# A graph network layer on one core: the last tile's packed slots are taken early and singly in one PSUM bank

## The reference

```python
msg = jnp.concatenate([h[src], h[dst]], axis=-1) @ Mw.T + Mb
s1, s2 = segment_sum(msg, dst), segment_sum(msg * msg, dst)
mx, mn = segment_max(msg, dst), segment_min(msg, dst)
mean = s1 / degc
var = relu(s2 / degc - mean * mean); std = sqrt(var + 1e-30)
agg = concatenate([mx, mn, std, var])
u = concatenate([h, agg, agg * (logd / 4), agg * (4 / logd)]) @ Uw.T + Ub
u = u * sqrt(1 / N); u = batchnorm(u) * bn_g + bn_b     # over all nodes
h = leaky_relu(u @ mix_w.T + mix_b) + h
h = elu(layernorm(h) * ln_g + ln_b)
```

## Time and profile before

| | |
|---|---|
| Median of 3 runs | 1823.03 us |
| The profiled execution's own time | 1825.5 us |
| Its span | 1823.8 us |
| Busy | POOL 1221.5, DVE 1085.2, PE 665.5, ACT 471.2 us |
| Line 676, gathers | 774 + 387, 948 ns each |
| Mean granted TensorE clock | 0.665 |

### The profile page before, as it was taken

The page is one execution under the profiler, slowest core; times in us unless marked ns, Lnnn a source line. Parts: engine busy times, 40 slices in busy tenths (PEclk is TensorE's granted clock), DMA queues, the critical chain, the costliest instruction groups (busy, mean ns, idle before and its releaser), DMA issues.

```text
span 1823.8 us, 10174 instructions
## 1 busy us (share of the span) xinstructions
PE 665.5 (36%) x2106; PEld 385.5 (21%) x2106; DVE 1085.2 (60%) x1980; ACT 471.2 (26%) x1029; POOL 1221.5 (67%) x1356
## 2 busy tenths in 40 slices
PE   5504444422222182434233222262543422222254
PEld 5403222211111141212111111131321211111122
DVE  8833766666555753666655555654566565655564
ACT  0106222222221155322122111146221211111125
POOL 3567777777777506777777777705777777777715
PEclk9856666666665695766656666686666666666577
DMA  7255344334444324333333334313333333334401
GB/s 73 56 136 163 106 108 108 106 107 108 109 110 133 87 78 117 106 107 107 106 107 109 108 110 127 112 47 119 112 107 108 106 107 109 107 107 124 118 26 36
DMA packets 98720, 188.61 MB, mean 103 GB/s; under 512 B 34326, under 2 KB 58598, under 8 KB 98654
## 3 DMA queue, kind: packets, MB, share of 16 engines
q0 software_dynamic: 59968, 160.68, 31.5%
q1 hardware_dynamic: 38691, 27.30, 6.3%
HBM read 169.15 MB, written 16.29 MB: 102 GB/s over the span
## 4 chain that ended last, share of the span: by engine, by line
POOL 48%; issue 20%; DVE 15%; PE 9%; ACT 4%; DMA 3%; SPq 0%; DVEq 0%; POOLq 0%; ACTq 0%
POOL G L676 45%; PE ps L829 3%; DVE ps L1294 3%; DVE ps L1295 2%; DVE ps L1296 2%; DMA G<-p_by_rank,index 1%; PE ps L814 1%; DVE tot L1396 1%; POOL shared_rows L662 1%; POOL rows_by_rank L620 1%; PE ps L826 1%; PE ps L868 1%; PE ps L767 1%; DVE agg L1398 1%; DVE agg L1400 1%
## 5 line engine op out<-in xcount | busy, mean ns | idle before, releaser
L676 POOL DMA_INDIRECT G<-p_by_rank,index x774 | 733.7, 948 | 355.3 <-issue 233.5
L1294 DVE TENSOR_TENSOR ps<-ps,G 128x1024 f32<-128x1024 f32 (+3 forms) x255 | 285.8, 1121 | 549.7 <-ACT ps L969 309.1
L676 POOL DMA_INDIRECT G<-p_by_node,index x387 | 367.1, 948 | 124.6 <-issue 115.2
L814 PE MATMUL ps<-wide_ident,agg 128*128 128x128 f32 x300 | 83.7, 435 | 901.7 <-ACT agg L982 901.7
L829 PE MATMUL ps<-w_u_sb,aggT 128*128 128x384 f32 x600 | 294.7, 652 | 0.0
L814 PEld LDWEIGHTS ps<-wide_ident,agg 128*128 128x128 f32 x300 | 53.7, 217 | 917.3 <-ACT agg L982 917.3
L829 PEld LDWEIGHTS ps<-w_u_sb,aggT 128*128 128x128 f32 x600 | 165.5, 276 | 153.6 <-issue 81.4
L975 ACT ACTIVATE msq<-tot,rdeg 128x128 f32<-128x128 f32 x75 | 30.1, 401 | 566.0 <-DVE tot L1396 529.3
L1296 DVE TENSOR_TENSOR ps<-ps,G 128x512 f32<-128x512 f32 (+3 forms) x255 | 161.9, 635 | 0.0
L1295 DVE TENSOR_TENSOR ps<-ps,G 128x512 f32<-128x512 f32 (+3 forms) x255 | 161.8, 635 | 0.0
L826 PE MATMUL ps<-w_own,hT 128*128 128x384 f32 x150 | 111.5, 847 | 0.0
(11 more groups left out here) (224 smaller groups left out, 1135.2 us busy)
## 6 DMA issues: line engine op xcount, KB each, us to landing
G<-p_by_rank,index POOLq DMA_INDIRECT x774, 2.8
G<-p_by_node,index POOLq DMA_INDIRECT x387, 2.8
p_by_rank<-base SPq DMA_DIRECT2D x12, 512.0 KB, 3.0
p_by_node<-G SPq DMA_DIRECT2D x6, 514.0 KB
w_u_sb<-in_w_u SPq DMA_DIRECT2D x3, 768.0 KB
x_r<-rows_by_rank SPq DMA_DIRECT2D x1, 1600.0 KB, 8.1
p_by_rank<-base SPq DMA_DIRECT2D x12, 128.0 KB, 3.3
windows<-src_pad SPq DMA_DIRECT2D x1, 1118.0 KB, 24.4
```

What stands on the lines that cost most here:

```text
L676: g.indirect_dma_start(G[:, n % R, j, 0:w], None, table, bass.IndirectOffsetOnAxis(ap=index[:, t, k0 + j:k0 + j + 1], axis=0))\
L814: ins = nc.tensor.transpose(ps[:, 2, i * D:(i + 1) * D], agg[:, t % 2, i * D:(i + 1) * D], ident[:, :])
L1294: TT(run[:, 0:nk, :], run[:, 0:nk, :], G[:, n % R, 0:nk, 0:2 * D], ALU.add)
```

## The change

The 10 packed slots of tile 24 are moved out of its groups into three groups of their own (4, 4 and 2 slots), which stand in `GROUPS` after tiles 6, 8 and 10, marked with -1 as their number in the tile. Tile 24's 17 gathered slots follow in groups of 4, 4, 4, 2, 1, 1 and 1. There are 113 groups, and still 387 gathers in the same order.

Tile 24 has no `begin`, no `own_rows` and no `close`. All its slots go through `take_singly`: three operations a slot into bank 5 (sums, maximum, minimum), each slot behind a wait for the one before. The first early slot starts from `base` in place of the bank. The last slot of all writes to `tot` and `agg`. On TensorE `update_last` stands in the place of `turn` and `update`: the own product first, then the two extremes turned into bank 2 as soon as they are there, then deviation and variance into bank 0. ScalarE copies each half by itself.

```diff
+    EARLY = {6 + 2 * i: (lo, min(lo + GW, TOP_SHARED)) for i, lo in enumerate(range(0, TOP_SHARED, GW))}
...
         if t == T - 1:
-            full, rest = divmod(PLAN[t] - 1, GW)
-            sizes = [GW] + [rest] * (rest > 0) + [GW] * (full - 1) + [1]
-        left, s0 = len(SHARED.get(t, ())), 0
+            full, rest = divmod(PLAN_T[t] - 3, GW)
+            sizes = [GW] * full + [rest] * (rest > 0) + [1] * 3
...
+        if t in EARLY:
+            lo, hi = EARLY[t]
+            own_slots.append(0)
+            shared_slots.append(range(lo, hi))
+            GROUPS.append((T - 1, -1, 0, hi - lo))
...
+            def update_last(l):
+                t, z = T - 1, ps[:, 4, 0:3 * D]
+                parts = (ps[:, 2, 0:2 * D], ps[:, 0, 0:2 * D])
...
+                mm(z, hT[:, hot(t)], w_own[:, :], start=True, stop=False)
+                pe.wait_ge(agg_copied.sem, agg_copied.at(l, t))
+                pe.wait_ge(low_ready.sem, low_ready.at(l, t + 1))
+                for i in range(2):
+                    ins = nc.tensor.transpose(parts[0][:, i * D:(i + 1) * D],
+                                              agg[:, t % 2, i * D:(i + 1) * D], ident[:, :])
+                ins.then_inc(half_turned.sem, 1)
+                pe.wait_ge(std_ready.sem, std_ready.at(l, t + 1))
+                for i in range(2):
+                    ins = nc.tensor.transpose(parts[1][:, i * D:(i + 1) * D],
+                                              agg[:, t % 2, (2 + i) * D:(3 + i) * D], ident[:, :])
+                ins.then_inc(agg_turned.sem, 1)
+                pe.wait_ge(half_copied.sem, half_copied.at(l, 1))
+                for i in range(4):
+                    if i == 2:
+                        pe.wait_ge(agg_copied.sem, agg_copied.at(l, t + 1))
+                    ins = mm(z, aggT[:, t % 2, i * D:(i + 1) * D], w_u_sb[:, i, :], start=False, stop=i == 3)
+                ins.then_inc(z_done.sem, 1)
...
-                    if n < NG and GROUPS[n][1] == 0:
+                    if n < NG and GROUPS[n][1] == 0 and GROUPS[n][0] < T - 1:
                         begin(l, GROUPS[n][0])
...
+            def take_singly(l, n):
+                t, j, _, nk = GROUPS[n]
+                sums, most, least = ps[:, 5, 0:2 * D], ps[:, 5, 2 * D:3 * D], ps[:, 5, 3 * D:4 * D]
+                into = sums, most, least
...
+                for i in range(nk):
+                    row = G[:, n % R, i, 0:2 * D]
+                    add = TT(into[0], sums, row, ALU.add)
...
+                    ch.step(add)
+                    ch.step(TT(into[1], most, row[:, 0:D], ALU.max))
+                    low_of = TT(into[2], least, row[:, 0:D], ALU.min)
+                    sums, most, least = into
+                    if i < nk - 1:
+                        ch.step(low_of)
+                        ch.wait()
+                low_of.then_inc(dve_used.sem, 1)
+                ch.wait()
+                dve.wait_ge(dve_used.sem, dve_used.at(l, n + 1))
```

More of the change, by code:

```diff
@@ L138, in build @@
     GROUPS, own_slots, shared_slots = [], [], []
+    TOP_SHARED = len(SHARED[T - 1])
+    EARLY = {6 + 2 * i: (lo, min(lo + GW, TOP_SHARED)) for i, lo in enumerate(range(0, TOP_SHARED, GW))}
+    PLAN_T = PLAN[:T - 1] + [OWN_K]
     for t in range(T):
-        full, rest = divmod(PLAN[t], GW)
+        full, rest = divmod(PLAN_T[t], GW)
         k0 = 0
@@ L144, in build @@
         if t == T - 1:
[L145 to L147 removed]
+            full, rest = divmod(PLAN_T[t] - 3, GW)
+            sizes = [GW] * full + [rest] * (rest > 0) + [1] * 3
+        left, s0 = len(SHARED[t]) if t in SHARED and t < T - 1 else 0, 0
         for j, nk in enumerate(sizes):
@@ L164, in build @@
         slot_before.append(slot_total[n % R])
-    tile_groups = [[n for n, g in enumerate(GROUPS) if g[0] == t] for t in range(T)]
+    tile_groups = [[n for n, g in enumerate(GROUPS) if g[0] == t and g[1] >= 0] for t in range(T)]
+    early_groups = [n for n, g in enumerate(GROUPS) if g[1] < 0]
     END = {tile_groups[t][-1]: t for t in range(T)}
-    CLOSE = {tile_groups[t][-1 - (t == T - 1)]: t for t in range(T)}
+    CLOSE = {tile_groups[t][-1]: t for t in range(T - 1)}
     CH = [(c, min(4, T - c)) for c in range(0, T, 4)]
@@ L1282, in accumulate @@
                     dve.wait_ge(brought[n].sem, brought[n].at(l, transfers(n)))
[L1283 to L1288, removed]
                 if j == 1:
@@ L1298, in accumulate @@
                     own_rows(l, n)
+            def take_singly(l, n):
+                t, j, _, nk = GROUPS[n]
+                sums, most, least = ps[:, 5, 0:2 * D], ps[:, 5, 2 * D:3 * D], ps[:, 5, 3 * D:4 * D]
+                into = sums, most, least
+                if n == early_groups[0]:
+                    sums, most, least = (base[:, t, S1:S2 + 1, :].rearrange("p a d -> p (a d)"),
+                                         base[:, t, TOP, :], base[:, t, LOW, :])
+                if n in END:
+                    dve.wait_ge(agg_turned.sem, agg_turned.at(l, t - 1))
+                    dve.wait_ge(var_ready.sem, var_ready.at(l, t - 1))
+                    into = tot[:, t % 2, :], agg[:, t % 2, 0:D], agg[:, t % 2, D:2 * D]
+                if n in brought:
+                    dve.wait_ge(brought[n].sem, brought[n].at(l, transfers(n)))
+                else:
+                    dve.wait_ge(gathered[n % R].sem, gathered[n % R].at(l, slot_before[n]))
+                for i in range(nk):
+                    row = G[:, n % R, i, 0:2 * D]
+                    add = TT(into[0], sums, row, ALU.add)
+                    if n in END:
+                        add.then_inc(summed.sem, 1)
+                        TT(into[1], most, row[:, 0:D], ALU.max).then_inc(dve_used.sem, 1)
+                        TT(into[2], least, row[:, 0:D], ALU.min).then_inc(low_ready.sem, 1)
+                        return
+                    ch.step(add)
[8 more added lines that the diff above has]
+                dve.wait_ge(dve_used.sem, dve_used.at(l, n + 1))
             def own_rows(l, n):
```

24 lines of the change are left out of this document (20 added, 4 removed).

## The result

| | median us | lowest to highest | runs |
|---|---|---|---|
| before | 1823.57 | 1822.81 to 1824.76 | 4 |
| changed | 1803.56 | 1803.44 to 1804.51 | 4 |

A forecast was written before the change was run, and what follows sets the result against it. It took POOL's 387 gathers a layer, 1.25 us each, as the bound, with the way from last gather to second half movable. 1825.5 - 16.8 - 3.2 = 1805.5, less 2.5 for the median: 1803.0 us, range 1799 to 1809.

The forecast's parts named there:

- VectorE's side: Tile 24, last gather to last slot: 4.0 us where it was 9.94, 9.63 and 9.24, gaining 16.8 us.
- TensorE's side: Tile 24's transposes and products: end 6.9 us after the last slot instead of 8.12, 7.98 and 7.79, gaining 3.2 us.
- One of the signs of being wrong: At tile 24, VectorE arriving later than its first group's landing would show the forecast wrong; no size was given.
- slots cost their full durations: Rival for tile 24's single slots on VectorE: 1.05 us each instead of 0.88, giving 1806.7 us; chance 0.10.
- The early groups: Packed slots after tiles 6, 8, 10: VectorE delayed 13 us a layer, the ring covers it, cost 0.
- The sum: Whole kernel: 1825.5 - 16.8 - 3.2 = 1805.5 us for the profiled execution, 2.5 less for the median, so 1803.0.

The follow-up runs named there:

- e3: The changed kernel with all three groups of packed slots after tile 23 instead of after tiles 6, 8 and 10; 1824.34 us, ratio 1.0004.
- e4: The changed kernel, packed slots still early, but tile 24 with begin, own rows and reductions, its gathered slots in groups of 4, 4, 4, 4, 1; 1812.16 us.
- e5: The changed kernel with tile 24's gathered slots taken singly in groups of 4, 4, 4, 4 and 1; 1812.65 us, ratio 0.9933.
- e1: The changed kernel with the old end of TensorE and ScalarE for tile 24 (own product between transposes and products, one copy); 1804.97 us, ratio 0.9892.
- e2: The kernel before with only the new end on TensorE and ScalarE (update_last and the copies by halves); 1823.34 us, ratio 1.0000.
- e8: The changed kernel with the packed groups after tiles 4, 5 and 6 instead of 6, 8 and 10; 1805.52 us, ratio 0.9889.
- e7: The changed kernel plus 6 unread products behind tile 24's own product and 2 in the wait for batch norm's factors; 1801.77 us, ratio 0.9871.
- e10: The changed kernel plus unread products: 8 behind the own product, a half-length one between transpose pairs, 2 before the second half; 2155.77 us in a slow group.
- e12: The changed kernel again, unaltered, in a group where the kernel before took 2173.68 us; 2166.25 us, ratio 0.9975.
- e9: The changed kernel with tile 24's gathered slots in groups of 4, 3, 3, 2, 1, 1, 1, 1, 1; 2165.13 us in a slow group, ratio 0.9961.

## Why the prediction was right

The time, 1803.0 forecast and 1803.56 measured, and the mechanism on VectorE's side both stand; on TensorE's side a term was missing. By steps:

- *VectorE's side.* Forecast 3 x 4.0 us from last gather to last slot and a gain of 16.8; measured 3.84 to 3.89, gain 17.2. The slot cost 0.86 to 0.87 us inside a group (0.88 forecast) and 0.92 as a group of its own. VectorE waited for the third group 3.49 us before the last gather's start (1721.23 to 1724.72), where the working had it 3.45 before. e3, e4 and e5 moved it by about what the same arithmetic gives (11.1 to 11.7 for 10.8, 6.45 for 6.6, 5.05 for 5.1). One of the signs of being wrong, VectorE coming to tile 24 later than its first group's landing, contradicted the working, which has 1727.6 for the landing and 1727.93 for VectorE. It came so by some 0.2 us (landing estimated at 1711.3, the gather's start at 1708.48 and 2.8 more; first slot at 1711.53), and cost nothing, as VectorE waited for the second and the third group.
- *Rival "slots cost their full durations".* Fell: the second operation starts 0.35 us after the first, whose duration is 0.43, the third 0.20 after one of 0.29. So a slot costs 0.87 instead of 1.05 us. The Trainium skill, "VectorE: DVE Perf Modes", section "The DRAIN you can't avoid", has besides the rule that the prediction used the remark that a next operation that is not held starts earlier. The prediction left it out; the trace agrees with the remark, and the rule without it doesn't hold for these shapes.
- *TensorE's side.* Transposes at 0.97 and 2.0 (0.86 and 2.0 forecast), products from 2.48 (2.6) to 7.0 (6.9), gain 2.9 (3.2). The clock rose later than assumed, 6.1 passes at 0.64 us and not 5.3, and the products began 0.1 earlier.
- *The step that was missing.* What TensorE does in the products was taken to end there. The second half starts behind them, and it lost 1.45 us in the profile (granted clock 0.80 and 0.56 in the last layer's windows, 1.00 and 0.71 before), so the TensorE part was worth about 1.5 us net in that execution and not 3.2. e1 and e2 show the same exchange (3.3 for 1.6, 2.3 for 2.75), e8 that it isn't there in each execution (20.6 and 151.9 against 24.0 and 151.8 before, 3.3 net, about what was forecast), e7 that an active TensorE in the gap ends it. The rule of "TensorE: Matmul & The Clock Gate" in the Trainium skill, Part 1, that recent activity lifts the clock, fits e7 and e10.
- *The early groups.* Cost 0 forecast, and 0 found: longest wait of POOL for VectorE 0.3 us in the changed kernel and in e8. The working behind it holds as well: where an early group stands, the next tile's begin ends 8.0 to 9.4 us after the variance (8.7 forecast), 4.3 before.
- *The sum.* 18.65 us of change (17.2 + 2.9 - 1.45) and 3.25 of the gathers' pace make 21.9 of the 22.0 between the spans. The forecast had 20.0 and took off 2.5 for the profiled execution being above the median. The working gave no reason for the 2.5. Before's profile is one with the longer gather interval, which is worth 3.25; whether the runs of the median had the shorter one isn't known, since they have no profile. That the medians differ by 20.0 and the terms give 18.65 lies within the ratio's interval of +-2.2 us.

What the forecast owes to luck is about 1.5 us: the loss in the second half, which it had not seen, lies within what such a measurement leaves. The forecast's gain of 20.0 is met by the medians, but by the terms of the profiles it is 18.65.

## What to carry to other kernels

In a kernel that is bound by a stream of issues, look at what stands between the last issue and the first thing that needs all of it: work that needs none of the stream's last pieces (packed slots, the own product) goes ahead of them, into time that a ring covers, and only then is it worth while to take the last pieces one by one; in the other order it cost 5.3 us here. Read the stretch behind the one that is shortened as well, and in more than one execution: here the second half started at the lower clock in 20 of 24 layers with the new end and in 1 of 6 with the old. An experiment on the clock needed work up to the start of the burst: with 2.8 us of idle behind a fill of 5.3 the products took 4.09 us, with 0.3 behind one of 7.0 they took 2.84.

## What was not expected of the hardware

- The gather's own duration has two values, 945 to 946 and 948 to 949 ns, one for a whole execution. In the rows of one view, second layer, the changed kernel's is above; this is e8's:

```profile
L687 POOL DMA_INDIRECT G<-p_by_rank,index x373 | 353.9, 949 | 113.7 <-issue 111.6 <-DVE ps L1337 1.2 <-DVE ps L1366 0.9
```

  Both values come on one chip (e10 949, e12 946). With 1161 gathers that is 3.3 us, as much as lies between the lowest and the highest of the 21 runs of before beside e1 to e4 (1821.68 to 1824.90); that it makes this spread isn't shown.
- In the group of e9 to e12 single operations take what they take elsewhere, and gathers are issued every 1.25 us while there is room, but there are waits that nothing explains. e12's waits, 250 to 1740 us, in the same columns as POOL's above:

```profile
ACT u_sb L1039 <- remote: 341.2, 27, 24.7
...
POOL G L687 <- DVE ps L1337: 159.7, 43, 16.1
DVE ps L1335 <- issue: 148.6, 26, 17.0
```

  and a piece of its timeline:

```profile
892.94 1.12 PE L849 MATMUL ps<-wide_ident,agg 128*128 128x128 f32 x4 [1.81 <-issue]
...
925.29 0.60 ACT L1033 ACTIVATE aggT<-ps 128x512 f32<-128x512 f32 x1 [32.40 <-remote]
```

  The transposes that line 1033 waits for end at 894.06, the copy starts 31 us later, and meanwhile VectorE waits for ScalarE and in the end the ring fills. Whatever delays it is not in the profile, and its cause stays open, also whether it belongs to a chip or to the time, as e5 to e8 carry the same chip number. POOL waited up to 16 us for VectorE there, and 20 us of gain became 7. That the gain hangs on the ring's slack fits with it, but the kernel before has no profile in that group to compare with.
